# Second attention of a six-layer kernel: four heads at a time in row and column groups of the array, masked by parity, in a written-out loop

## The chip, the cores and the metric

One core of a Trainium2 chip. Times are device microseconds of that core. TensorE (PE) multiplies on a 128 x 128 array and writes PSUM, eight banks of 128 partitions by 2 KB. VectorE (DVE), ScalarE (ACT) and GpSimd (POOL) do the rest; GpSimd works on SBUF alone. SyncE (SP) issues the transfers.

## The reference, cut to what matters

```python
x = x + 0.5 * L0_ffn(layernorm(x))
x = x + L0_attn(layernorm(x))
x = x + 0.5 * L0_ffn(layernorm(x))
x = x + 0.5 * L1_ffn(layernorm(x))
x = x + L1_attn(layernorm(x))        # the second attention
x = x + 0.5 * L1_ffn(layernorm(x))

# L1_attn: B, S, E, H = 4, 256, 512, 32; D = E // H = 16
q, k, v = split(x @ qkv_w + qkv_b)            # each b, s, H, 16
q, k = rope(q), rope(k)
s = einsum('bqhd,bkhd->bhqk', q, k) / 4 + (1 - tril) * -66504
p = softmax(s)
y = einsum('bhqk,bkhd->bqhd', p, v).reshape(b, s, e) @ out_w + out_b
```

x is 4 batches x 256 tokens x 512; all is fp32. The second attention has 4 x 32 = 128 heads of 16 columns.

## The kernel before

The six layers run one after another on x, which stays in SBUF. Each engine has its own instruction list; semaphores order them. Large products run in three fp32r matmuls (`product`, L346: high x high, high x low, low x high) on operands split into a high and a low half; scores, weighted sums and transposes are plain fp32.

The second attention (`b_tensor`, `b_scalar`, `b_vector`, `b_gpsimd`) begins when the feed-forward layer has written all of x. A batch has 256 tokens in two tiles of 128, and 32 heads in four groups of eight (a group is 128 columns of q, k and v). Per batch there are six projections `PROJ` (q, k, v by two token tiles, 12 matmuls each), a bias addition for each (L1564), and for q and k a rotation: cosine on VectorE (L1570), sine on GpSimd (L1675), sum on VectorE (L1578). Per group, `b_tensor_prepare` (L1375) transposes q and k into one bank and VectorE copies them to `qkT` (L1584). ScalarE then makes eight copies of the transposed q, each multiplied by a column of `table` that is one on the 16 partitions of one head and zero elsewhere (`qz`, L1470), and scatters v on the diagonal of a zeroed buffer `vz` (L1481), so that each head's product over all 128 partitions is that head's own.

Head i passes through the engines in steps j: scores(j) (L1396: query tile 0 against 128 keys, tile 1 against 256), minima on VectorE with the causal mask added (L1602, L1605; scores are negated), exponentials with row sums on ScalarE (L1495), the inverse sums a step later (L1612), two products on GpSimd (L1688, L1690), three 128 x 128 transposes three steps later (L1405, into bank PT), a copy to SBUF on VectorE (L1616), and the weighted sum four steps later (L1416, L1418), in which a group's eight heads accumulate into bank OB. A group's result is split by ScalarE (L1502) and VectorE (L1620). TensorE's order within a step is turn(j-3), scores(j), weigh(j-4), then extra work from tables: the next group's transposes, a norm of the next batch, one projection of the next batch at j = 19, 21, ... 29, output products (L1431) at j = 34 to 36. `b_run` runs batches in a loop of the hardware (`Fori`), with 37 steps written out at its start and for the last batch. Banks 0 and 1 take projections and transposed q and k, 2 and 3 scores, 4 the turned probabilities, 5 the weighted sum, 6 and 7 norms and outputs.

In the last batch the weights of the next layer are split as well (L245 on ScalarE, L258 on GpSimd), 11 chunks over 28 steps.

Of the kernel before, what the change touches and what calls it, by code (L numbers as in the profile page):

```python
# [24 lines left out]
P = 128  # L25
# [60 lines left out]
T_FIRST = T_HEAD + HG1  # L86
# [14 lines left out]
def constants():  # L101
# [22 lines left out]
    t[:, T_HEAD:T_HEAD + HG1] = np.arange(P)[:, None] // D1 == np.arange(HG1)[None, :]  # L124
# [4 lines left out]
def program(nc, x_in, w_in, table_in, bias_in, rows_in, out):  # L129
    ctx = ExitStack()  # L130
    with ctx:
# [44 lines left out]
        with ExitStack() as a:  # L176
            qkT = sb(a, "qkT", [P, 2, 2 * SEQ])
# [3 lines left out]
            oT1 = [sb(a, f"oT1_{i}", [P, GR1, SEQ], F32R) for i in (HI, LO)]  # L181
            qkv = sb(a, "qkv", [P, 2, 3 * DIM])
            s1 = sb(a, "s1", [P, 4, 3 * P])
            bqkv = sb(a, "bqkv", [P, 3 * DIM])
# [1077 lines left out]
        b_proj_free = sem("b_proj_free")  # L1262
        b_sin = sem("b_sin")
        b_cos = sem("b_cos")
        b_rope = sem("b_rope")
        b_q = sem("b_q")
        b_v = sem("b_v")
# [6 lines left out]
        b_pt = sem("b_pt")  # L1274
# [3 lines left out]
        b_out = sem("b_out")  # L1278
        b_added = sem("b_added")
        b_zero = sem("b_zero")  # L1280
        LN1 = 32
        TURN_LAG, WEIGH_LAG = 3, 4
        OVER = WEIGH_LAG + 1

        PROJ = [(0, 0), (1, 0), (0, 1), (1, 1), (2, 0), (2, 1)]
        PROJ_AT = {19 + 2 * i: p for i, p in enumerate(PROJ)}
        FILLS1 = GR1 + len(PROJ)


        LN_AT, LAST_LN_AT = {5: 0, 12: 1}, {5: 0, 11: 1, 17: 2, 24: 3}  # L1290
        LAST_SPLIT_AT = {OVER + i * 28 // F1_CHUNKS: i for i in range(F1_CHUNKS)}
        NEXT_AT = 28
        OUTPUTS_AT = {34: [0, 1], 35: [2], 36: [3]}

        def prep_at(j):


            return j // HG1 + 1 if j % HG1 == 0 and j // HG1 % GR1 < GR1 - 1 else None

        def ended_before(j):  # L1300

            i = j - 1 - WEIGH_LAG
            return i // HG1 if i > 0 and i % HG1 == HG1 - 1 else None

        def fill_of(b, what):


            if isinstance(what, int):
                i = what // GR1 * FILLS1 + what % GR1 - 1
            else:  # L1310
                i = GR1 - 1 + FILL_ORDER.index(what)
            n = FILLS1 - 3 + i
            return b * FILLS1 + n, n % 2

        NEXT = "next"
        FILL_ORDER = PROJ[:5] + [NEXT] + PROJ[5:]

        def b_run(eng, step, ahead):

            ahead(-1)  # L1320
            for j in range(OVER):
                step(0, j, True)
            with eng.Fori(0, BATCH - 1) as b:
                for j in range(OVER, HEADS1 + OVER):
                    step(b, j, True)
            for j in range(OVER, HEADS1 + OVER):
                step(BATCH - 1, j, False)

        def there(i, more):

            return 0 <= i and (i < HEADS1 or more)

        def ln_no(b, tt):
            return b * 2 + (LN1 + 2 + tt)


        def b_tensor(pe):
            pe.wait_ge(f_mul, ffn1b.m0)
            st_a1.ready(pe, A1_CHUNKS - 1)
            b_run(pe, lambda b, j, more: b_tensor_step(pe, b, j, more),  # L1340
                  lambda b: b_tensor_ahead(pe, b))

        def b_claim(pe, b, what):
            n, s = fill_of(b, what)
            pe.wait_ge(b_proj_free, n + 1)
            return bank[s]

        def tile_at(j, more):

            return (LN_AT if more else LAST_LN_AT).get(j)  # L1350

        def b_tensor_norm(pe, b, tt):
            pe.wait_ge(b_added, b * 4 + 1)
            ln_turn(pe, ln_no(b, tt), tt % 2, OUTB[tt % 2])

        def b_tensor_project(pe, b, what):
            j, tt = what
            if what == PROJ[0]:
                pe.wait_ge(ln_done, ln_no(b, 1) + 1)
            dst = b_claim(pe, b, what)  # L1360
# [6 lines left out]
        def b_tensor_prepare(pe, b, what):  # L1367
            grp = 0 if what == NEXT else what
            if what == NEXT:
                pe.wait_ge(b_rope, b * 4 + 8)  # L1370
            dst = b_claim(pe, b, what)
            for j in range(2):
                for tt in range(2):
                    c = j * DIM + grp % GR1 * P
                    last = nc.tensor.transpose(dst[:, j * SEQ + tt * P:j * SEQ + (tt + 1) * P],  # L1375
                                               qkv[:, tt, c:c + P], ident)
            last.then_inc(b_proj, 1)

        def b_tensor_ahead(pe, b):
            for what in FILL_ORDER:  # L1380
                if what == NEXT:
                    b_tensor_prepare(pe, b, NEXT)
                else:
                    b_tensor_project(pe, b, what)

        def b_tensor_step(pe, b, j, more):
            def scores(i):
                grp, hh = divmod(i, HG1)
                s = grp % 2
                if hh == 0:  # L1390
                    n = fill_of(b + grp // GR1 - 1, NEXT) if grp % GR1 == 0 else fill_of(b, grp)
                    pe.wait_ge(b_proj_free, n[0] + 3)
                    pe.wait_ge(b_q, b * GR1 + grp + 1)
                pe.wait_ge(b_min, b * HEADS1 + i + 1)
                for qt, n in enumerate((P, 2 * P)):
                    last = nc.tensor.matmul(bank[2 + i % 2][:, qt * P:qt * P + n],  # L1396
                                            qz[:, s, hh, qt * P:(qt + 1) * P],
                                            qkT[:, s, SEQ:SEQ + n], start=True, stop=True)
                last.then_inc(b_scores, 1)

            def turn(i):
                pe.wait_ge(b_norm, b * HEADS1 + i + 1)
                pe.wait_ge(b_pt, b * HEADS1 + i + 1)
                for blk in range(3):
                    last = nc.tensor.transpose(bank[PT][:, blk * P:(blk + 1) * P],  # L1405
                                               s1[:, i % 4, blk * P:(blk + 1) * P], ident)
                last.then_inc(b_turned, 1)

            def weigh(i):
                grp, hh = divmod(i, HG1)  # L1410
                if hh == 0:
                    pe.wait_ge(b_v, b * GR1 + grp + 1)
                    pe.wait_ge(b_o_lo, b * GR1 + grp + 1)
                pe.wait_ge(b_pt, b * HEADS1 + i + 2)

                nc.tensor.matmul(bank[OB][:, 0:SEQ], vz[:, grp % 2, 0, hh, :], pt1[:, i % 2, 0:2 * P],  # L1416
                                 start=hh == 0, stop=False)
# [452 lines left out]
```

## Time and profile before

| | us |
|---|---|
| median of 3 runs | 2020.61 |
| lowest, highest | 2018.2, 2024.47 |
| span of the profiled execution | 2014.8 |
| PE, PEld busy in it | 1872.6, 1655.0 |
| DVE, ACT, POOL busy in it | 1174.6, 1104.2, 881.5 |
| second attention (1575.8 to 1941.3) | 365.5 |

The profile is of one execution; its own time is known as the span from its first to its last instruction, 2014.8, which lies 3.4 us under the lowest run and 5.8 under the median. A matmul record's duration includes the way through the array; how fast matmuls follow each other is read from the chain. An fp32 matmul of scores or weighted sum is two records (256 calls, 512 records).

### The profile page before, as it was taken

What the parts mean: (1) busy time and instruction counts of PE and PEld (TensorE: products, weight loads), DVE (VectorE), ACT (ScalarE), POOL (GpSimd) and SP (SyncE); (2) the same over time, 40 slices, a digit from 0 to 9 for tenths busy, and PEclk for the clock granted to TensorE, in tenths of its full rate; (3) what the DMA queues carried; (4) which work ended last, traced back from release to release, by engine and by line L of the source; (5) the groups of instructions that cost most, each with busy time, mean ns of one, the idle gap of its engine ahead of it and who ended that gap; (6) DMA issues with size and microseconds to landing.
All of it is one profiled execution on the core that took longest, in us unless ns stands there. A gap on an engine that the chain in (4) does not pass through costs nothing.

```text
span 2014.8 us, 35562 instructions
## 1 busy us (share of the span) xinstructions
PE 1872.6 (93%) x11076; PEld 1655.0 (82%) x11076; DVE 1174.6 (58%) x3502; ACT 1104.2 (55%) x3103; POOL 881.5 (44%) x1241
## 2 busy tenths in 40 slices
PE   5979999999999999999999999998988898989888
PEld 4769998988988988988998899997766687878776
DVE  3555565565565466456456556545557675766766
ACT  3336566565566566466656656664325455465744
POOL 5335444444544444444544544542313353545630
PEclk9999999999999999999999999999989999999999
DMA  5200011021011012002002001102111100000101
GB/s 173 68 1 17 17 54 34 7 64 34 1 53 49 1 41 62 1 29 69 6 17 70 17 17 53 33 7 63 37 41 49 42 1 1 0 1 0 38 6 42
DMA packets 35013, 66.12 MB, mean 33 GB/s; under 512 B 3968, under 2 KB 4096, under 8 KB 34816
## 3 DMA queue, kind: packets, MB, share of 16 engines
q1 hardware_dynamic: 34816, 63.74, 10.4%
q8 instruction: 94, 1.54, 0.3%
q14 instruction: 103, 0.84, 0.1%
HBM read 61.62 MB, written 2.10 MB: 32 GB/s over the span
## 4 chain that ended last, share of the span: by engine, by line
PE 76%; DVE 8%; ACT 7%; issue 7%; POOL 2%; DMA 0%; DVEq 0%; ACTq 0%; SPq 0%; POOLq 0%
PE bank L346 56%; PE bank L925 5%; PE bank L912 4%; PE bank L1396 3%; PE bank L927 2%; PE bank L1416 2%; ACT s L1026 2%; PE bank L1405 2%; PE bank L1418 1%; ACT W L245 1%; ACT s L1495 1%; POOL WF L258 1%; DVE h L634 1%; DVE x L1183 1%; PE bank L318 1%
## 5 line engine op out<-in xcount | busy, mean ns | idle before, releaser
L346 PE MATMUL bank<-W,oT 128*128 128x512 f32 x1632 | 434.2, 402 | 0.0
L1224 POOL TENSOR_TENSOR qk<-work,qk 128x512 fp32r<-128x512 f32 (+1 forms) x160 | 189.8, 1186 | 489.7 <-ACT qk L1017 489.7
L346 PEld LDWEIGHTS bank<-W,oT 128*128 128x128 f32 x1632 | 289.4, 190 | 47.5
L1033 ACT COPY pt<-bank 128x384 f32<-128x384 f32 x256 | 121.9, 476 | 342.5 <-PE bank L912 342.0
L1026 ACT ACTIVATE s<-s,neg_max 128x128 f32<-128x128 f32 (+1 forms) x512 | 227.5, 445 | 59.2 <-DVE neg_max L1137 57.7
L1216 POOL TENSOR_TENSOR work<-work,table 128x512 f32<-128x512 f32 (+1 forms) x160 | 160.6, 1004 | 138.4 <-ACT work L1012 138.4
L1495 ACT ACTIVATE s<-s,neg_max 128x128 f32<-128x128 f32 (+1 forms) x256 | 114.3, 447 | 136.8 <-DVE neg_max L1605 136.4
L346 PE MATMUL bank<-W,xnA 128*128 128x320 f32 (+1 forms) x1056 | 186.7, 333 | 1.6 <-DVE qkv L1564 0.8
L1114 DVE TENSOR_TENSOR work<-bank,table 128x512 f32<-128x512 f32 (+1 forms) x160 | 101.9, 637 | 131.7 <-ACT work L1012 131.7
L346 PEld LDWEIGHTS bank<-W,xnA 128*128 128x128 f32 x1056 | 166.4, 188 | 14.2 <-DVE qkv L1564 1.3
L346 PE MATMUL bank<-xnA,W 128*128 128x256 f32 (+1 forms) x1080 | 163.6, 302 | 11.8 <-DVE W L251 6.4
L346 PE MATMUL bank<-qk 128*128 128x256 f32 (+1 forms) x768 | 167.7, 354 | 5.6 <-POOL qk L1224 5.6
L346 PE MATMUL bank<-xnB,W 128*128 128x256 f32 (+1 forms) x1080 | 161.8, 300 | 4.7 <-DVE xnB L331 4.7
L925 PE MATMUL bank<-pt,lvv 128*128 128x256 f32 x512 | 152.8, 379 | 13.1 <-DVE oT L1150 12.4
L1189 DVE COPY lvv<-bank 128x320 f32<-128x320 f32 x128 | 62.9, 492 | 171.8 <-PE bank L346 171.8
L346 PEld LDWEIGHTS bank<-xnA,W 128*128 128x128 f32 x1080 | 143.6, 192 | 21.5 <-DVE W L251 9.5
L1237 POOL TENSOR_TENSOR s<-s,inv_sum 128x256 f32<-128x256 f32 x256 | 156.9, 613 | 0.0
L346 PEld LDWEIGHTS bank<-xnB,W 128*128 128x128 f32 x1080 | 143.1, 191 | 11.5 <-DVE xnB L331 5.6
L912 PE MATMUL bank<-table,s 128*128 128x128 f32 x768 | 126.8, 274 | 9.8 <-issue 8.4
L1017 ACT CAST qk<-work 128x512 fp32r<-128x512 f32 (+1 forms) x160 | 92.4, 578 | 73.3 <-DVE work L1123 72.4
L1235 POOL TENSOR_TENSOR s<-s,inv_sum 128x128 f32<-128x128 f32 x256 | 107.9, 422 | 52.5 <-DVE inv_sum L1145 51.6
L1123 DVE TENSOR_TENSOR work<-work 128x512 f32<-128x512 f32 (+1 forms) x160 | 113.2, 708 | 30.2 <-issue 15.0
(107 smaller groups left out, 3913.3 us busy)
## 6 DMA issues: line engine op xcount, KB each, us to landing
raw<-in_weights SPq DMA_DIRECT2D x215, 256.0 KB, 2.8
x<-in_x SPq DMA_DIRECT2D x8, 256.0 KB, 4.8
out<-x SPq DMA_DIRECT2D x8, 256.0 KB, 2.0
row<-in_bias_rows SPq DMA_DIRECT2D x5, 256.0 KB, 2.7
table<-in_constants SPq DMA_DIRECT2D x1, 960.0 KB, 5.1
bqkv<-in_bias_rows SPq DMA_DIRECT2D x1, 768.0 KB, 4.8
table<-in_constants SPq DMA_DIRECT2D x1, 69.0 KB, 2.4
biases<-in_bias_columns SPq DMA_DIRECT2D x1, 15.0 KB, 2.9
```

Of the source, the lines that this page charges most:

```text
L346: last = nc.tensor.matmul(out_ap, lhs(i), rhs(j), start=start and k == 0, stop=stop and k == 2)
L912: last = nc.tensor.transpose(bank[PT][:, blk * P:(blk + 1) * P], s0[:, s, blk * P:(blk + 1) * P], ident)
L925: nc.tensor.matmul(bank[OB][:, 0:SEQ], lvv[:, 0, col:col + P], pt0[:, k, 0:2 * P], start=True, stop=False)
L1026: last = nc.scalar.activation(s0[:, s, cols], s0[:, s, cols], ACT.Exp, bias=neg_max[:, s, qt:qt + 1], scale=-1.0, accum_out=row_sum[:, s, ...
L1033: nc.scalar.copy(pt0[:, k, :], bank[PT][:, 0:3 * P]).then_inc(a_pt, 1)
L1114: nc.vector.tensor_tensor(work[:, 2 + s, cols], bank[fs][:, cols], table[:, T_COS + cols.start:T_COS + cols.stop], ALU.mult).then_inc(a_pr ...
L1123: nc.vector.tensor_tensor(work[:, 2 + s, cols], work[:, 2 + s, cols], work[:, s, cols], ALU.add).then_inc(a_rope, 1)
L1216: nc.gpsimd.tensor_tensor(work[:, s, cols], work[:, s, cols], table[:, T_SIN + cols.start:T_SIN + cols.stop], ALU.mult).then_inc(a_sin, 1)
L1224: nc.gpsimd.tensor_tensor(lo, work[:, 2 + s, st.columns(what)], hi.bitcast(F32), ALU.subtract).then_inc(a_rope_lo, 1)
L1235: nc.gpsimd.tensor_tensor(s0[:, s, 0:P], s0[:, s, 0:P], inv_sum[:, s, 0:1].to_broadcast([P, P]), ALU.mult)
L1237: nc.gpsimd.tensor_tensor(s0[:, s, P:3 * P], s0[:, s, P:3 * P], inv_sum[:, s, 1:2].to_broadcast([P, 2 * P]), ALU.mult).then_inc(a_norm, 1)
L1495: last = nc.scalar.activation(s1[:, s, cols], s1[:, s, cols], ACT.Exp, bias=neg_max[:, s, qt:qt + 1], scale=-1.0, accum_out=row_sum[:, s, ...
```

## The change

The second attention is written anew, everything else stays. A step is now four heads (a quad, half a group: the even heads of a group or its odd heads); there are 8 quads a batch, 32 in all and two steps to finish, written out for all batches, without `Fori`.

- Scores: q of a group is copied twice instead of eight times, once with the odd and once with the even heads zeroed. Head j of the quad lies on partitions 32j to 32j+31 (its 16 and 16 zeroed ones), and its scores are a matmul over those 32 partitions alone, on row group j, into its own bank j. The four heads' matmuls for query tile 0 come first, then the four for tile 1.
- Weighted sum: v of a head is 32 columns (16 of them zero), on column group j, into partitions 32j to 32j+31 of bank OUT1.
- The zeroed buffer `vz` shrinks from 8 to 2 slots a group and tile, and GpSimd fills it instead of ScalarE. The two products of a head on GpSimd become one of 384 columns, with the inverses written out per block by VectorE, one reciprocal for two heads. Three of four copies of turned probabilities move from VectorE to ScalarE. The addition of the bias row moves from VectorE to GpSimd.
- The turned probabilities have two banks (4, 5). Projections, transposed q and k, norms and output products all go through the one bank FILL (7), in a fixed order: each waits until its predecessor has been copied out.
- The rotation is done in place; q and k of two batches are kept.

```diff
-            qz = sb(a, "qz", [P, 2, HG1, SEQ])
-            vz = sb(a, "vz", [P, 2, 2, HG1, P])
-            pt1 = sb(a, "pt1", [P, 2, 3 * P])
+            qz = sb(a, "qz", [P, 2, 2, SEQ])
+            vz = sb(a, "vz", [P, 2, 2, 2, P])
+            pt1 = sb(a, "pt1", [P, 4, 3 * P])
...
+        SCORE, PTB, OUT1, FILL = (0, 1, 2, 3), (4, 5), 6, 7
+        PROJ_STEP = {1: 0, 2: 1, 3: 2, 4: 3, 7: 4}
+        def middle_use(n):
+            b, s = divmod(n, PER_BATCH)
+            if n >= QUADS:
+                return None
+            if s == 0:
+                return ("proj", b, 5)
+            if s in PROJ_STEP and b + 1 < BATCH:
+                return ("proj", b + 1, PROJ_STEP[s])
+            if s in (5, 6) and b > 0:
+                return ("out", b - 1, s - 5)
+            return None
+        def first_use(n):
...
+            if s == 0:
+                return ("norm", b, 0)
+            if s == 2 and b + 1 == BATCH:
+                return ("norm", b, 2)
+            if s in (1, 3, 5):
+                return ("prep", b, s // 2 + 1)
+            if s == 6 and b + 1 < BATCH:
+                return ("prep", b + 1, 0)
+        def last_use(n):
...
+            if s == 0:
+                return ("norm", b, 1)
+            if s == 2 and b + 1 == BATCH:
+                return ("norm", b, 3)
...
+            def scores():
+                group, odd = divmod(n, 2)
...
+                at_least(pe, b_min, 4 * n)
+                for qt in range(2):
+                    cols = slice(qt * P, qt * P + (qt + 1) * P)
+                    for j in range(4):
+                        last = nc.tensor.matmul(bank[SCORE[j]][:, cols],
+                                                qz[rows(j), group % 2, odd, qt * P:(qt + 1) * P],
+                                                kT[rows(j), group % 2, 0:(qt + 1) * P], start=True, stop=True)
                 last.then_inc(b_scores, 1)
+            def weigh(m):
+                group, odd = divmod(m, 2)
...
+                for s in b_pt:
+                    pe.wait_ge(s, 2 * (m + 1))
+                for tt in range(2):
+                    for j in range(4):
+                        last = nc.tensor.matmul(bank[OUT1][rows(j), tt * P:SEQ],
+                                                vz[:, group % 2, odd, tt, 32 * j:32 * (j + 1)],
+                                                pt1[:, j, tt * 2 * P:(tt + 2) * P],
+                                                start=odd == 0 and tt == 0, stop=odd == 1 and tt == 1)
...
+            if n < QUADS:
+                scores()
+            if n >= 2:
+                weigh(n - 2)
+            b_tensor_fill(pe, first_use(n))
+            if 1 <= n <= QUADS:
+                turn(n - 1, 0)
+                turn(n - 1, 1)
+            b_tensor_fill(pe, middle_use(n))
+            if 1 <= n <= QUADS:
+                turn(n - 1, 2)
+                turn(n - 1, 3)
+            b_tensor_fill(pe, last_use(n))
...
+            if n >= 2 and n % 2:
...
+                act.wait_ge(b_pv, group + 1)
+                nc.scalar.copy(oT1[HI][:, group % ORING, :], bank[OUT1][:, 0:SEQ]).then_inc(b_o_hi, 1)
+            if here:
+                exponentials(0)
+            if first and first[0] == "norm":
+                norm_hi(first)
+            if before:
+                b_pt_copy(act, n - 1, 0)
+            if first and first[0] == "prep":
+                b_scalar_masks(act, *first[1:])
+            if here:
+                exponentials(1)
+            if before:
+                b_pt_copy(act, n - 1, 1)
+            if here:
+                exponentials(2)
+                exponentials(3)
+            if before:
+                b_pt_copy(act, n - 1, 2)
...
```

VectorE's step is minima of heads 0 and 1, the copy of a group's transposed keys, minima of heads 2 and 3, then the low half of a group's result, a norm's low half, the cosine, inverses(0) (heads 0 and 1), the rotation's sum, norm moments, the bias addition or the addition of an output product, norm applications, inverses(1) (heads 2 and 3), the copy of turned head 3 of the quad before. GpSimd's step is products 0 and 1, norm powers, a sine, a group's values, products 2 and 3, a bias row, weight splits.

## Rows read from the trace of the kernel before

**Rows 1.** Windows: start of the second attention, all of it, what follows; us, PE, PEld, DVE, ACT, POOL busy (x), PEclk, DMA.
```profile
...
1575.80:1597.10 21.30, 17.62 (x77) 13.70 (x77) 12.13 (x16) 3.45 (x10) 12.17 (x10) 1.00 0.27 99
1575.80:1941.30 365.50, 325.31 (x1896) 281.67 (x1896) 247.17 (x923) 199.50 (x710) 183.84 (x311) 0.99 0.04 12
1941.30:2014.80 73.50, 61.99 (x262) 47.95 (x262) 50.63 (x84) 32.63 (x53) 3.70 (x4) 0.97 0.09 33
...
```

**Rows 2.** Waits in 1575.8 to 1941.3: engine line <- releaser: total, times, longest.
```profile
...
POOL s L1688 <- DVE inv_sum L1612: 162.9, 102, 8.9
ACT s L1495 <- DVE neg_max L1605: 136.4, 115, 4.6
...
DVE s L1602 <- PE bank L1396: 26.0, 62, 2.8
...
```

**Rows 3.** The chain, four stretches of the stage: start us, us, what.
```profile
...
1692.29 2.72 issue
...
1703.08 0.45 PE bank L1375 x4
...
1713.37 0.33 PE bank L1405 x3
1713.70 0.66 PE bank L1396 x4
1714.36 0.43 PE bank L1416 x2
1714.79 0.22 PE bank L1418 x2
...
1726.20 2.77 PE bank L346 x12
...
```

**Rows 4.** Groups by shape in 1575.8 to 1941.3: count | busy us, mean ns | idle before.
```profile
...
L1690 POOL TENSOR_TENSOR s<-s,inv_sum 128x256 f32<-128x256 f32 x128 | 84.1, 657 | 0.0
...
L346 PE MATMUL bank<-W,xnA 128*128 128x512 f32 x288 | 71.2, 398 | 1.1 <-DVE qkv L1564 0.8 <-DVEq L1533 0.3
...
L1396 PEld LDWEIGHTS bank<-qkT,qz 128*128 128x128 f32 x512 | 68.6, 195 | 9.9 <-issue 7.8 <-DVE qkv L1564 1.9 <-DVE neg_max L1605 0.2
...
L1470 ACT ACTIVATE qz<-qkT,table 128x256 f32<-128x256 f32 x128 | 60.2, 496 | 24.4 <-DVE qkT L1584 24.4
...
L1688 POOL TENSOR_TENSOR s<-s,inv_sum 128x128 f32<-128x128 f32 x128 | 53.3, 417 | 163.1 <-DVE inv_sum L1612 162.9
...
L1396 PE MATMUL bank<-qkT,qz 128*128 128x128 f32 x256 | 50.7, 280 | 8.4 <-ACT qz L1470 6.7 <-DVE qkv L1564 1.5 <-issue 0.2
...
L258 POOL TENSOR_TENSOR W<-raw,W 128x512 fp32r<-128x512 f32 x11 | 14.0, 1272 | 5.8 <-ACT W L245 5.8
...
L245 ACT CAST W<-raw 128x512 fp32r<-128x512 f32 x11 | 6.7, 606 | 0.0
...
```

**Rows 5.** Timeline of one head's minima and exponentials: start us, us, engine.
```profile
...
1705.32 0.28 DVE L1602 CUSTOM_DVE_ANT_0 s<-bank,table 128x128 f32<-128x128 f32 x1
...
1705.87 0.16 DVE L1612 RECIPROCAL inv_sum<-row_sum 128x2 f32<-128x2 f32 x1
...
1705.99 0.40 ACT L1495 ACTIVATE s<-s,neg_max 128x128 f32<-128x128 f32 x1 [0.43 <-DVE neg_max L1605]
...
1706.88 0.49 ACT L1470 ACTIVATE qz<-qkT,table 128x256 f32<-128x256 f32 x1
...
```

**Rows 6.** The page, part 5: the same copy of turned probabilities in the first attention.
```profile
...
L1033 ACT COPY pt<-bank 128x384 f32<-128x384 f32 x256 | 121.9, 476 | 342.5 <-PE bank L912 342.0
...
```

**Rows 7.** Windows of TensorE alone, 1673 to 1682, 1930 to 1932: us, PE busy (x), PEclk.
```profile
...
1673.60:1675.70 2.10, 0.00 (x0) 1.00 0.00 0
1676.50:1679.90 3.40, 3.40 (x15) 0.50 0.00 0
1680.00:1682.00 2.00, 2.00 (x14) 1.00 0.04 12
1930.00:1932.00 2.00, 0.58 (x5) 1.00 0.01 4
...
```

More of the change, by code:

```diff
@@ L85 @@
 T_HEAD = T_MH + 2
[L86 removed]
+T_FIRST = T_HEAD + 2
 T_M0 = T_FIRST
@@ L1315, in program @@
[L1315 to L1331, printed above, removed]
@@ L1337, in b_tensor, with proj_bank, prep_bank @@
+        def proj_bank(b, i):
+            return bank[(0, 1, 2, 3, 0)[i]] if b == 0 and i < 5 else bank[FILL]
+        def prep_bank(b, g):
+            return bank[1] if b == 0 and g == 0 else bank[FILL]
         def b_tensor(pe):
@@ L1339, in b_tensor, with b_tensor_project @@
             st_a1.ready(pe, A1_CHUNKS - 1)
[L1340 to L1360, printed above, removed]
+            for i in range(5):
+                if i == 4:
+                    pe.wait_ge(b_biased, 1)
+                b_tensor_project(pe, 0, i)
+            pe.wait_ge(b_biased, 2)
+            b_tensor_prepare(pe, 0, 0)
+            for n in range(STEPS1):
+                b_tensor_step(pe, n)
+            fill_released(pe, ("out", BATCH - 1, 0))
+            b_tensor_out(pe, BATCH - 1, 0, bank[FILL])
+            b_tensor_out(pe, BATCH - 1, 1, bank[SCORE[0]])
+        def b_tensor_project(pe, b, i):
+            j, tt = PROJ[i]
+            pe.wait_ge(ln_done, LN1 + 2 * b + tt + 1)
+            dst = proj_bank(b, i)
             for c in range(KC):
@@ L1490, in b_scalar_step, with b_scalar_masks @@
[L1490 to L1493 removed]
+            b_scalar_masks(act, 0, 0)
+            for n in range(STEPS1):
+                b_scalar_step(act, n)
+        def b_scalar_masks(act, b, g):
+            group = GR1 * b + g
+            act.wait_ge(b_k, group + 1)
+            for odd in range(2):
+                last = nc.scalar.activation(qz[:, group % 2, odd, :], prep_bank(b, g)[:, 0:SEQ], ACT.Copy,
+                                            scale=table[:, T_HEAD + odd:T_HEAD + odd + 1])
+            last.then_inc(b_q, 1)
@@ L1519, in b_scalar_step, with norm_hi @@
-            if more and 0 <= j - NEXT_AT - 1 < 3:
-                i = j - NEXT_AT - 1
-                b_scalar_queries(act, b, NEXT, range(3 * i, min(3 * i + 3, HG1)))
-            if more and j == NEXT_AT + 3:
-                b_scalar_values(act, b, NEXT)
+            def norm_hi(use):
+                kind, b, i = use
+                ln_hi_part(act, norm_no(b, i), FILL, xn_tile(i))
+            first, last = first_use(n), last_use(n)
+            here, before = n < QUADS, 1 <= n <= QUADS
@@ new lines, in b_vector_step @@
+            first, middle, last = first_use(n), middle_use(n), last_use(n)
+            roped = middle_use(n - 1) if n else None
+            roped = roped if roped and roped[0] == "proj" and roped[2] < 4 else None
+            here, before = n < QUADS, 1 <= n <= QUADS
+            if here:
+                minima(0)
+                minima(1)
+            if first and first[0] == "prep":
+                b_vector_keys(dve, *first[1:])
+            if here:
+                minima(2)
+                minima(3)
@@ new lines, in b_vector_step @@
+            if here:
+                inverses(0)
+            if roped:
+                b_vector_turned(dve, *roped[1:])
+            if norms_after(n):
+                b_vector_moments(dve, *norms_after(n))
+            if middle and middle[0] == "proj":
+                b_vector_biased(dve, *middle[1:])
+            if middle and middle[0] == "out":
+                b_vector_added(dve, *middle[1:], bank[FILL])
+            if norms_after(n):
+                b_vector_apply(dve, *norms_after(n))
@@ L1658, in b_gpsimd @@
+            if here:
+                inverses(1)
+            if before:
+                b_pt_copy(dve, n - 1, 3)
+            if last:
+                norm_lo(last)
         def b_gpsimd(pool):
```

528 lines of the change are left out of this document (252 added, 276 removed).

## The prediction

> **What bounds the stage now.** The diff touches only the second attention, so I first cut it out with the view by windows. It runs from 1575.8 to 1941.3, 365.5 us of the span of 2014.8; the 73.5 us behind it and the 1575.8 ahead of it keep their code [rows 1]. In it TensorE is busy 325.3 us, VectorE 247.2, ScalarE 199.5, GpSimd 183.8, at a granted clock of 0.99. Next the waits: GpSimd waits 162.9 us for the inverses, ScalarE 136.4 for the minima, VectorE 26.0 for the scores [rows 2]. All three wait for what comes from TensorE. The chain shows why: a head costs TensorE 0.33 us (three transposes), 0.66 (two score matmuls), 0.43 and 0.22 (weighted sum), 1.64 in all, one head right behind the other [rows 3]. 128 heads are 210 us; 24 projections and 8 output products (12 matmuls each [rows 4], 2.76 us [rows 3]) are 88; transposes of queries, keys and norms some 12. That is 310 of the 365.5. The other 55 are the start (21.3 [rows 1], of which 16.6 projections), waits at the change of a group, and loop ends, one of which stands in the chain as 2.72 us of "issue" [rows 3].
>
> **What TensorE gains.** Four heads now share the array: eight score matmuls on row groups 32j, eight weighted-sum matmuls on column groups 32j. The count does not fall: per head still two of each. What falls is time only if neighbours in different groups run at once. No matmul on a part of the array is in this trace, so I bound it.
> - No overlap: scores 4 x 0.66 = 2.6 us for four heads, weighted sum the same, as now.
> - Full overlap: 0.66 each, the time of one.
> - Between: the profile shows two matmul records for each fp32 matmul written (512 weight records for 256 calls [rows 4], and as many matmuls), so each group gets two in a row. If TensorE takes them strictly in order, the second record of group j holds up group j+1 until the first has streamed: only this second and the next group's first overlap. Four groups then take 5 beats instead of 8: 5/8 x 2.6 = 1.6 us.
>
> I take 1.6 for each, as it needs no reordering and is near the middle. The Trainium skill (TensorE: Matmul & The Clock Gate, Part 3) says that matmuls start and end in program order and that four row tiles of one matmul each gave 3.07x; by that figure scores and sum would take some 0.85 each. It gives no such figure for fp32 in two records; no row here shows either.
>
> Three times a step the array changes its division. A 128-column record lasts 0.28 us [rows 4] where the transposes follow each other at 0.11 [rows 3], so emptying the array may cost 0.17, 0.5 a step; nothing is the other bound. I take 0.5, since the trace has no reason why it should be free. The Trainium skill (TensorEngine Tiling (Array Packing), Tiling Modes) says that a change of mode drains TensorE, which speaks against this change. With the drain the sum below stands as it is; without one it would be some 12 us lower (25 steps by 0.5).
>
> TensorE's work for a quad is then 1.77 + 1.77 + 12 transposes 1.32 + 0.17 = 5.0 us (6.6 before).
>
> **What the other engines need.** ScalarE: exponentials of one head take 0.89 (start to start [rows 5]), so 3.6 for four; three of four copies of the turned probabilities move to it, 3 x 0.48 [rows 6]; together 5.0. The eight masked query copies of a group (0.49 each [rows 4]) become two; the copies of the values go to GpSimd. VectorE: minima 0.55 a head [rows 5], 2.2, one copy 0.55, two inverses 0.3, and the rotation. GpSimd: 128 and 256 columns take 0.42 and 0.66 [rows 4], by that slope 384 in one take 0.9; 3.6 a step, plus sines (1.9 a projection), value copies, row additions: up to 7.7 in the fullest step, 5.5 on average. Its products are wanted only a step later, so it stays hidden under 7 us and more. If its cover goes (steps of 6), the fullest cost 1.7 more. What is queued behind the new waits: on TensorE, the projection's wait for FILL holds the transposes of heads 2 and 3 and the next scores, for which VectorE waits; on ScalarE, the wait for the weighted sum holds the exponentials.
>
> **The steps.** 32 steps of four heads. Let 0 be the start of the weighted sum of two steps ago; minima start about there too. The critical order is: probabilities of head 0 copied out by ScalarE behind exponentials 0, then exponentials 1, copy, exponentials 2 and 3; then inverses and the last copy on VectorE (0.7), which releases the next weighted sum and stands ahead of the next minima.
> - Empty even step: exponentials 0 end 1.55; turned at 1.77 + 0.33 + 0.27 = 2.4; copy 2.85, exponentials 3.75, copy 4.2, two more 6.0, plus 0.7: 6.7 us. Odd: ScalarE has the group's result (0.35) ahead of exponentials 0 and waits there for the weighted sum (1.95): 7.55.
> - With a projection or output product and nothing else TensorE sets it: 5.0 + 2.8 = 7.9.
> - With the next group's queries as well (three or four steps in eight): they go into the one bank FILL, and the projection waits until ScalarE has written both masked copies. In an odd step: exponentials 0 end 3.25, copy 3.7, masks 4.6; TensorE has nothing from 2.9 to 4.65; projection 7.4, transposes 8.1, scores 9.9. Even: 9.5. Without a projection 8.45 and 8.05.
> - Step 0 of a batch: transposed norm, its two copies, projection, its bias addition (6.9 to 7.55), second norm, all through FILL: 9.9. Step 7: both norms' moments and applications stand ahead of VectorE's second inverses, and their power behind GpSimd's products: 9.2.
>
> A middle batch: 9.9 + 9.9 + 7.9 + 9.9 + 7.9 + 9.9 + 9.5 + 9.2 = 74.2. The first has no output products and no sums in its first two steps: 68.7. The last has few projections, but two more norms and the 11 weight splits, now in seven steps (1.0 us of ScalarE and 2.0 of GpSimd in each, by 0.61 and 1.27 [rows 4], behind their work of the step; SP's loads wait for them as before, and no other transfer moves): 70. Start: the first scores wait for four biased and rotated projections (4 x 2.8, a sine of 1.9, rotation, transposes, masks): 18 instead of 21.3. End: two steps without scores, two output products (5.5), addition: 14. Sum 18 + 68.7 + 148.4 + 70 + 14 = 319 us against 365.5: 46 less. Writing the loop out removes its ends, which is in these numbers. The profiled span of 2014.8 lies 5.8 under the median of the runs, 2020.6; that rest stays. Forecast 2020.6 - 46 = 1974.
>
> **Rivals.**
> - *Full overlap.* In some 25 steps that TensorE sets, 2 x 0.95 goes, in 7 others 0.9, at the end 1.9: 56 us more, 1918. For it: moving columns are the whole cost of a matmul here. Against: two records a group in order. With steps of 6 to 8 us TensorE is under half busy in some, so part may come back as clock. The Trainium skill (TensorEngine Tiling (Array Packing), Overview) states up to 4x for a small dimension of 32 or less, which speaks for this one.
> - *No overlap, the change does not do what it says.* Scores and sum cost 2.6 each: 2.0 more in the 25 steps, 1.2 in the others, 59 more: 378, slower by 12, 2033. It ends on the other side: TensorE's work is then that of today, and FILL's waits are added to it. It decides once scores and sum cost over 2.4 each. For it: fp32 comes in several passes, whose weights may not be loadable beside a running group (weight records of 0.19 us [rows 4] for matmuls of 0.11 apart).
> - *The clock.* After 2.1 us without a matmul the granted clock was 0.50 for 3.4 us, 1.2 in place of 2.4 GHz [rows 7]; a head then took about 3.3 us instead of 1.64. The new steps have gaps of 1 to 1.7 us in FILL's waits and 1 to 2 in empty steps. Ten falls at 2 us: +20, 1994; in every step +60, which would eat the gain. Against: after two microseconds with 0.58 us of matmuls in them it stayed at 1.00 [rows 7]. The twelve emptiest steps are the risk.
> - *VectorE, not TensorE, is late* (sequence of inverses and copies, wait for FILL longer than seen): 0.5 us a step, +16, 1990. The Trainium skill (TensorEngine Tiling (Array Packing), Performance Considerations) expects this: after tiling, the copies out of PSUM may set the pace. In the empty steps above they do.
>
> **How the numbers follow.** Pairwise overlap as summed: 0.45 (its own range 1950 to 2000). Full or nearly full: 0.25 (1895 to 1950). No overlap: 0.15 (2015 to 2050). Clock or late VectorE on top: 0.15 (1985 to 2015). A measurement of this kernel tells about 0.3%, 6 us. Faster: 0.45 + 0.25 + 0.13 = 0.83; slower 0.13, same 0.04. The range reaches from the full overlap into no overlap: 1900 to 2030 leaves out the ends of both, under 2 in 10.
>
> **What would show it.** In the new profile: the stage under 325 us; the eight score records of 128 columns over 0.55 us (0.86 without overlap, 0.22 with all of it), those of 256 over twice that; TensorE idle before projections in steps with queries, released by ScalarE's masks; ScalarE's idle before exponentials falling from 137 us to under 60; no row of loop ends. Wrong it would be if the records of neighbouring groups stand one behind the other, if the clock in the stage falls under 0.95, or if GpSimd's products release TensorE's transposes in most steps.

## The result and the profile after

The changed kernel takes 1936.4 us (median of four runs, 1935.3 to 1938.3) against 2020.1 for the kernel before on the same chip (2018.2 to 2024.5): ratio 0.960, 95% interval 0.958 to 0.962. The profiled execution has a span of 1934.2 us and a time of 1936.0. The forecast was 1974 with a range of 1900 to 2030; faster was right, the gain is 84 us where 46 were forecast. One run of the kernel before (5135.0 us) and one of values_first (2246.1) stand far above all others and are left out of every ratio and of the median of values_first.

First the stage by windows in the changed kernel (its first 20 us, all of it, what follows; columns as in [rows 1]):

```profile
...
1578.70:1599.00 20.30, 14.84 (x65) 11.78 (x63) 12.48 (x20) 0.94 (x3) 8.79 (x10) 0.89 0.30 104
...
1578.70:1862.50 283.80, 229.56 (x1897) 168.15 (x1895) 176.79 (x756) 183.13 (x678) 169.29 (x223) 0.90 0.05 15
1862.50:1934.20 71.70, 60.55 (x262) 46.81 (x262) 50.55 (x84) 32.63 (x53) 3.71 (x4) 1.00 0.09 34
...
```

283.8 us instead of 365.5: the stage has 81.7 of the 84. TensorE is busy 229.6 us where it was 325.3, with 1897 matmul records in place of 1896. Its granted clock fell from 0.99 to 0.90; with 0.5 as the lower of the two levels that is 0.1 / 0.5 = 0.2 of the stage, some 57 us at 1.2 GHz.

The groups by shape in the stage show what the records of the new form and the moved work cost:

```profile
...
L1440 PE MATMUL bank<-kT,qz 32*128 32x256 f32 x256 | 21.4, 406 | 0.0
L1440 PE MATMUL bank<-kT,qz 32*128 32x128 f32 x256 | 17.0, 337 | 1.5 <-ACT qz L1495 1.5
...
L1454 PE MATMUL bank<-pt,vz 128*32 128x128 f32 x256 | 15.4, 309 | 0.0
...
L1749 POOL TENSOR_TENSOR s<-s,b_inv_sum 128x384 f32<-128x384 f32 x128 | 107.4, 860 | 83.4 <-DVE b_inv_sum L1662 83.0
...
L1760 POOL COPY vz<-v 128x128 f32<-128x128 f32 x32 | 8.6, 299 | 0.0
...
L1502 ACT COPY pt<-bank 128x384 f32<-128x384 f32 x96 | 45.1, 469 | 17.3 <-PE bank L1465 17.2
...
```

256 score records with a mean of 337 ns, and yet only 17.0 us of busy time: 256 x 0.337 would be 86. One record takes no less time than before (280 ns in [rows 4]); several of them run at the same moment. In the step whose scores start at 1640.72 four score records are under way at 1640.76 and eight at 1640.96, by windows of 1 ns.

The timeline of TensorE alone in one step of the second batch (start, length, engine and line, count of records):

```profile
...
1687.91 0.82 PE L1465 MATMUL bank<-table,s 128*128 128x128 f32 x6
1688.65 0.94 PE L1440 MATMUL bank<-kT,qz 32*128 32x128 f32 x16
1689.52 0.86 PE L1454 MATMUL bank<-pt,vz 128*32 128x256 f32 x16
1690.31 0.66 PE L1399 MATMUL bank<-table,qkB 128*128 128x128 f32 x4
1690.80 0.82 PE L1465 MATMUL bank<-table,s 128*128 128x128 f32 x6
1692.86 3.02 PE L350 MATMUL bank<-W,xnA 128*128 128x512 f32 x12 [1.24 <-ACT qz L1495]
...
```

Start to start, the scores of four heads take 0.87 us and the weighted sum 0.79; before, that was 4 x 0.66 and 4 x 0.65 [rows 3]. The last row is the wait that the forecast described: the queries go through FILL, and the projection stands 1.24 us behind ScalarE's masked copies.

Waits in the stage (in total, times, longest):

```profile
...
POOL s L1749 <- DVE b_inv_sum L1662: 83.0, 43, 4.4
...
ACT s L1509 <- DVE b_neg_max L1654: 27.2, 17, 2.6
...
PE bank L350 <- ACT qz L1495: 13.6, 11, 1.4
PE bank L1454 <- DVE pt L1502: 13.3, 14, 2.1
...
DVE s L1651 <- PE bank L1440: 8.9, 19, 0.9
...
```

ScalarE waited 136.4 us for minima and now waits 27.2, VectorE waited 26.0 for scores and now 8.9 [rows 2]. Instead TensorE waits: for the masks, and for the turned probabilities. The chain through a step without a projection (step 5 of the first batch, its steps counted from 0) shows who sets the pace there:

```profile
...
1641.90 0.89 PE bank L1454 x16
1642.82 0.38 ACT oT L1523
1643.19 0.88 ACT s L1509 x4
1644.07 0.36 ACT pt L1502
1644.43 0.74 ACT qz L1495 x2
1645.18 0.86 ACT s L1509 x4
1646.04 0.37 ACT pt L1502
1646.41 1.77 ACT s L1509 x8
1648.32 0.52 DVE pt L1502
...
1648.97 1.45 PE bank L1454 x16
...
```

Of 7.07 us between two of TensorE's rows, 5.4 are ScalarE's: the copy of a group's result, exponentials, copies of turned probabilities and masked queries, one behind the other. 0.5 are VectorE's last copy. TensorE is no longer the bound in such a step. In the step ahead of it, which has a projection and no queries, TensorE waits only 0.24 us: the two engines are nearly even there.

### The profile page after: what moved, and what is told of

It is laid out like the page before. It is cut to its first block, busy times and chain, and to the rows that moved or that the text cites. A ratio compares the mean times of both kernels' runs of the same rounds, so it can differ in the third digit from the quotient of the medians.

```text
span 1934.2 us, 34615 instructions
## 1 busy us (share of the span) xinstructions
PE 1773.3 (92%) x11076; PEld 1539.3 (80%) x11076; DVE 1106.9 (57%) x3334; ACT 1088.1 (56%) x3071; POOL 899.9 (47%) x1153
## 4 chain that ended last, share of the span: by engine, by line
PE 71%; ACT 9%; DVE 8%; issue 6%; POOL 3%; DMA 1%; DVEq 0%; ACTq 0%; SPq 0%; POOLq 0%
PE bank L350 56%; PE bank L929 5%; PE bank L916 4%; PE bank L931 2%; ACT s L1509 2%; ACT s L1030 2%; PE bank L1454 1%; ACT W L249 1%; PE bank L322 1%; PE bank L1465 1%; DVE x L1187 1%; POOL WF L262 1%; POOL rstd L315 1%; DVE work L649 1%; DVE h L638 1%
## 5 line engine op out<-in xcount | busy, mean ns | idle before, releaser
L1030 ACT ACTIVATE s<-s,neg_max 128x128 f32<-128x128 f32 (+1 forms) x512 | 227.7, 446 | 51.0 <-DVE neg_max L1141 50.2
L1220 POOL TENSOR_TENSOR work<-work,table 128x512 f32<-128x512 f32 (+1 forms) x160 | 191.9, 1200 | 134.3 <-ACT work L1016 134.3
L350 PE MATMUL bank<-W,xnA 128*128 128x320 f32 (+1 forms) x1056 | 190.9, 338 | 11.9 <-ACT qz L1495 7.7
L350 PEld LDWEIGHTS bank<-xnB,W 128*128 128x128 f32 x1080 | 143.2, 191 | 11.4 <-DVE xnB L335 5.6
L1749 POOL TENSOR_TENSOR s<-s,b_inv_sum 128x384 f32<-128x384 f32 x128 | 107.4, 860 | 83.4 <-DVE b_inv_sum L1662 83.0
```

Of the source, the lines that this page charges most:

```text
L350: last = nc.tensor.matmul(out_ap, lhs(i), rhs(j), start=start and k == 0, stop=stop and k == 2)
L1030: last = nc.scalar.activation(s0[:, s, cols], s0[:, s, cols], ACT.Exp, bias=neg_max[:, s, qt:qt + 1], scale=-1.0, accum_out=row_sum[:, s, ...
L1220: nc.gpsimd.tensor_tensor(work[:, s, cols], work[:, s, cols], table[:, T_SIN + cols.start:T_SIN + cols.stop], ALU.mult).then_inc(a_sin, 1)
L1749: nc.gpsimd.tensor_tensor(blocks, blocks, b_inv_sum[:, at, 1:4].unsqueeze(2).to_broadcast([P, 3, P]), ALU.mult).then_inc(b_norm, 1)
```

## The experiments

All runs, each against the kernel before on its own chip (there 2018.5 to 2022.8 us); the stage is that of the profiled execution, from its first projection to the first matmul behind it.

| kernel | median us | ratio to before, 95% interval | stage us | clock in stage |
|---|---|---|---|---|
| before | 2020.1 | 1 | 365.5 | 0.99 |
| changed | 1936.4 | 0.960 (0.958 to 0.962) | 283.9 | 0.90 |
| full_both | 2027.2 | 1.004 (1.001 to 1.006) | 374.7 | 0.97 |
| full_scores | 1975.9 | 0.978 (0.973 to 0.982) | 323.4 | 0.94 |
| full_sums | 1995.4 | 0.987 (0.982 to 0.992) | 346.2 | 0.94 |
| by_head | 1939.7 | 0.960 (0.956 to 0.964) | 286.5 | 0.89 |
| written_out | 2010.7 | 0.995 (0.992 to 0.997) | 359.2 | 1.00 |
| warm | 1930.4 | 0.956 (0.952 to 0.960) | 277.3 | 0.98 |
| early | 1927.7 | 0.954 (0.950 to 0.958) | 272.5 | 0.92 |
| early_warm | 1921.1 | 0.950 (0.945 to 0.954) | 267.6 | 0.99 |
| after_again | 1934.9 | 0.959 (0.957 to 0.961) | 283.9 | 0.90 |
| early_again | 1924.3 | 0.955 (0.952 to 0.957) | 270.0 | 0.94 |
| early_warm_start | 1922.2 | 0.952 (0.950 to 0.954) | 272.6 | 0.92 |
| values_first | 1917.0 | 0.949 (0.946 to 0.953) | 266.2 | 0.98 |

### Does the gain come from groups that run at once?

The first theory is that nearly all of the gain is that matmuls in different groups of the array run together; the rival, that the order of the steps and the loop written out bring it. Three kernels put the scores, the weighted sum or both back on the whole array, with the same number of matmuls and moving columns; the operands are then four times as high or wide, and a quad's eight sums accumulate in one place, with `start` at the first and `stop` at the last:

```
-  qz[rows(j), group % 2, odd, qt * P:(qt + 1) * P], kT[rows(j), group % 2, 0:(qt + 1) * P]
+  qz[:, group % 2, odd, qt * P:(qt + 1) * P], kT[:, group % 2, 0:(qt + 1) * P]      # full_scores
-  bank[OUT1][rows(j), tt * P:SEQ], vz[:, group % 2, odd, tt, 32 * j:32 * (j + 1)]
+  bank[OUT1][:, tt * P:SEQ], vz[:, group % 2, odd, tt, :]                           # full_sums
```

**full_both**

> Scores and weighted sums are issued on the whole array again (128 partitions, 128 columns), as many matmuls as in the changed kernel and in the same order; scores become sums over the heads of a quad and the weighted sum lands on all partitions, so the values differ. Theory A, the gain comes from groups of the array running at once: the eight matmuls of the scores take 2.6 us again instead of 0.77, those of the sums 2.6 instead of 0.7; TensorE needs 9.3 us in a step with a projection; the stage takes 350 to 370 us and the program 2000 to 2020. Theory B, the gain comes from the rest (loop written out, copies and products moved, no group changes): the stage stays under 310 us, the program under 1960.

**full_scores**

> Only the scores are on the whole array again (values differ as they then sum over the quad's heads). Theory A: 1.9 us more in each of some 22 steps in which TensorE has a projection or an output product, nearly nothing in the others, since the scores are issued ahead: 1936 + 40 = 1976 us. Theory B: within 10 us of 1936.

**full_sums**

> Only the weighted sums are on the whole array again (each head's sum lands on all partitions, so values differ). Theory A: the sum stands in the chain of every step (copies, sum, transposes, copies), so 1.9 us more in nearly all 32: 1936 + 50 to 60 = 1990 us, more than for the scores. Theory B: within 10 us of 1936.

With both on the whole array the kernel takes 2027.2 us, 0.4% more than before, and its stage 374.7, both somewhat over what was expected of the groups' theory. Put back alone, the scores give 1975.9 (40 more than the changed kernel) and the weighted sum 1995.4 (59 more). TensorE's timeline of full_both in a step without a projection:

```profile
...
1649.17 0.38 PE L1466 MATMUL bank<-table,s 128*128 128x128 f32 x2
1649.39 2.79 PE L1440 MATMUL bank<-kT,qz 128*128 128x128 f32 x16
1652.02 2.78 PE L1454 MATMUL bank<-pt,vz 128*128 128x256 f32 x16
1654.63 0.60 PE L1399 MATMUL bank<-table,qkB 128*128 128x128 f32 x4
...
```

Start to start 2.63 and 2.61 us for what takes 0.87 and 0.79 in groups: 1.76 and 1.82 less a step. At most three of these score records are under way at once, looked at every 0.08 us. In the stage, scores in groups are worth 374.7 - 346.2 = 28.5 us as long as the sum is on the whole array, the sum 374.7 - 323.4 = 51.3, and both together 90.8, or 2.84 for each of 32 steps. That is more than their sum. Most of the excess stands in the step at the start of a batch: step 0 of the second batch takes 12.3 us in full_both and still 12.3 in full_sums, 10.3 in full_scores and 9.0 in the changed kernel. Why it does was not tried. The order of the steps without the groups brings nothing; the rival of the experiment falls.

### Does the order in which the matmuls are issued matter?

The forecast took 1.6 us for four heads because each group has two records in a row, and a strict order would let only neighbours overlap. by_head makes the runs longer: the loops over heads and query tiles change places, so that each group has four records in a row.

```
-                for qt in range(2):
-                    for j in range(4):
+                for j in range(4):
+                    for qt in range(2):
```

> The scores are issued head by head (tile 0 then tile 1 of a head, then the next head), so that each row group gets four records in a row instead of two. If TensorE took matmuls strictly in order, only the last record of a head could overlap the first of the next: 4 x 0.64 - 3 x 0.11 = 2.2 us for the scores of a quad instead of 0.77, and the program about 30 us longer, 1966. If each group takes its own matmuls as it becomes free, the scores still take 0.8 us and the program 1936, within 6.

The kernel takes 1939.7 us, the same ratio as the changed kernel, and the scores as long:

```profile
...
1640.49 0.38 PE L1465 MATMUL bank<-table,s 128*128 128x128 f32 x2
1640.80 0.96 PE L1440 MATMUL bank<-kT,qz 32*128 32x128 f32 x16
...
```

0.96 us against 0.94. If a group's later records held up the next group, this order would cost clearly more than the other. The strict order in groups falls: in this kernel, how many records of one group stand in a row (two or four) makes no difference that shows.

### What is the loop, written out, worth?

written_out is the kernel before with its loop over the batches unrolled and nothing else changed.

```
-            with eng.Fori(0, BATCH - 1) as b:
+            for b in range(BATCH - 1):
```

> This is the kernel before with its loop over the batches written out and nothing else changed. The theory that writing the loop out is a small part of the gain: the chain of waits of the kernel before shows a loop end as 2.72 us of issue; two or three of them go, so 5 to 8 us less, about 2013 to 2015. The rival, from the run with whole-array scores and sums (2027.2 against 2020.1, that is all of the gain lies in the groups running together): the loop ends lie under work of other engines or TensorE's queue runs ahead over them, so within 0.3% of 2020.

The ratio is 0.995 (0.992 to 0.997), some 11 us, and the stage is 359.2 us instead of 365.5, so 6.3 less in the stage; the rest lies ahead of it or is spread of the runs, and its cause stays open. The theory holds in size, and the forecast read its row rightly: the kernel before has two such loop ends (2.72 and 2.76 us in the chain), in which VectorE stands for 2.3 us with nothing named that it waits for, and written_out has neither:

```profile
...
1784.36 0.56 DVE L1616 COPY pt<-bank 128x384 f32<-128x384 f32 x1 [2.33 <-issue]
...
```

Behind them the kernel before ran at half clock for some 3 us each (0.51 in 1697.4 to 1700.4); written_out has no such stretch there. Another wait stays in both kernels, once a batch, where the first scores of a new batch are due. In the profile of the kernel before TensorE waits 2.23 us for ScalarE's masked queries; in that of written_out the wait has no name, but TensorE starts 0.1 us behind the last of the same copies:

```profile
...
1675.75 0.99 PE L1396 MATMUL bank<-qkT,qz 128*128 128x128 f32 x4 [2.23 <-ACT qz L1470]
...
1765.67 0.89 ACT L1470 ACTIVATE qz<-qkT,table 128x256 f32<-128x256 f32 x2
...
1766.67 0.89 PE L1396 MATMUL bank<-qkT,qz 128*128 128x128 f32 x4 [2.20 <-issue]
...
```

The first row is of the kernel before, the others are of written_out. Against this kernel, full_both costs 374.7 - 359.2 = 15.5 us in the stage. So the edit is two things: groups, worth 91 us, and a new order of work with masks and FILL, which costs 15 and gets 6 back from the loop.

### What does the lower clock cost?

TensorE ran at 1.2 GHz for some 57 us of the changed kernel's stage. The longest stretch is at the start, where TensorE waits for the first rotated queries. The window on it, and the rows of TensorE's timeline there:

```profile
...
1594.50:1608.00 13.50, 7.31 (x32) 5.20 (x33) 8.07 (x30) 6.22 (x20) 3.27 (x5) 0.50 0.00 0
...
```

```profile
...
1596.40 1.09 PE L1399 MATMUL bank<-table,qkB 128*128 128x128 f32 x4 [3.96 <-DVE qkB L1606]
1599.03 1.67 PE L1440 MATMUL bank<-kT,qz 32*128 32x128 f32 x16 [1.54 <-ACT qz L1495]
1600.77 1.09 PE L322 MATMUL bank<-table,work 128*128 128x128 f32 x4
1604.53 4.68 PE L350 MATMUL bank<-W,xnA 128*128 128x512 f32 x12 [2.67 <-DVE xnA L335]
...
```

warm adds 42 matmuls (84 records) that nobody reads into TensorE's waits, so that the clock stays up:

```
+        def b_tensor_warm(pe, count, to=OUT1):
+            for _ in range(count):
+                nc.tensor.matmul(bank[to][:, SEQ:SEQ + 256], ident, table[:, T_M1:T_M1 + 256],
+                                 start=True, stop=True)
...
+            b_tensor_warm(pe, 8)      # ahead of the first turned queries
...
+            if n < 2:
+                b_tensor_warm(pe, 6 if n == 0 else 2)
```

> The kernel after, with some 70 matmuls of 256 columns that nobody reads, put into TensorE's waits of the emptiest steps and of steps 0 and 1. In the kernel after TensorE's granted clock is 0.90 in the stage, some 57 us of it at half. The theory that the half clock costs time: the granted clock in the stage rises to 0.97 or more and the stage (283.8 us) gets 8 to 15 us shorter, 1922 to 1928 in all. The rival that it lies in waits and costs nothing: the clock rises and the time stays within 6 us of 1936, or gets longer by what the added matmuls hold up (up to 10 us).

The clock in the stage rises to 0.98, the stage is 277.3 us, 6.6 less (8 to 15 were expected), and the kernel takes 1930.4. The interval of its ratio overlaps that of the changed kernel, so the whole time alone does not decide; the steps do. In the same place, in warm:

```profile
...
1600.19 0.94 PE L1451 MATMUL bank<-kT,qz 32*128 32x128 f32 x16 [0.24 <-ACT qz L1523]
...
1605.70 3.02 PE L350 MATMUL bank<-W,xnA 128*128 128x512 f32 x12 [0.54 <-DVE xnA L335]
...
```

The projection takes 3.02 us instead of 4.68, and step 0, from one start of scores to the next, 9.9 instead of 11.6, step 1 7.7 instead of 9.3. In the second batch nearly nothing changes (7.8, 7.2, 7.8, 5.9 against 7.8, 7.1, 7.8, 5.9), and in the last the added matmuls make two steps longer (by 1.3 and 1.7 us) and three shorter (by 0.4 to 1.4). So the half clock costs where a projection is on the path, and hardly anything in steps that ScalarE sets. The third batch fits this: its step 0, which holds a projection, takes 10.3 us in warm, and 11.2 in the changed kernel, where the clock fell in it.

### What does the wait for the masks cost?

early sends the turned queries and keys of groups 2 and 3 and of the next batch's group 0 as the last use of FILL in an even step, behind its projection instead of ahead of the next one, and puts their copies first in the next step of VectorE and ScalarE.

```
-            if s in (1, 3, 5):
-                return ("prep", b, s // 2 + 1)
...
+            if s == 2:
+                return ("prep", b, 2)
+            if s == 4:
+                return ("prep", b, 3)
...
+            earlier = last_use(n - 1) if n else None
+            if earlier and earlier[0] == "prep":
+                b_scalar_masks(act, *earlier[1:])
```

> The kernel after, with the transposed queries and keys of groups 2 and 3 and of the next batch's group 0 sent as the last use of FILL in the step before, and the masked copies first in ScalarE's next step. TensorE's wait for ScalarE's masked copies ahead of a projection (up to 1.4 to 1.6 us, 11 of them) goes. The theory that this wait lies on the path: 10 to 15 us less, 1921 to 1926. The rival that ScalarE and VectorE set these steps and TensorE only waits elsewhere: within 6 us of 1936; ScalarE's exponentials then start 1 us later in the steps with masks.

> Both edits of the two runs before in one kernel. If both costs lie on the path and do not overlap, the gains add: 18 to 30 us less than the kernel after, 1906 to 1918. If the early queries leave longer empty waits and the clock falls there, the added matmuls are worth more here than alone; if neither lies on the path, 1930 to 1946.

early takes 1927.7 us, and the stage 272.5, 11.4 less. TensorE's waits for the masked copies ahead of projections are 3 with 3.8 us in all, where they were 11 with 13.6, and the projection follows the transposes at once:

```profile
...
1683.90 0.86 PE L1462 MATMUL bank<-pt,vz 128*32 128x256 f32 x16
1684.68 0.87 PE L1473 MATMUL bank<-table,s 128*128 128x128 f32 x6
1685.32 3.01 PE L350 MATMUL bank<-W,xnA 128*128 128x512 f32 x12
1688.16 0.82 PE L1473 MATMUL bank<-table,s 128*128 128x128 f32 x6
...
```

early_warm, with both edits, takes 1921.1 and its stage 267.6: 16.3 less than the changed kernel, where the edits alone give 6.6 and 11.4. They nearly add (18.0), but the kernel takes 3 us more than the upper end of what was expected for it (1906 to 1918).

To compare on one chip, three kernels ran together: the changed one, early, and early with added matmuls only ahead of and in steps 0 and 1.

> The changed kernel itself once more, so that the three kernels of this call can be compared on one chip: 1936 us within 0.3%.

> The kernel with the queries and keys sent a step early, beside the changed kernel on the same chip. If the waits for the masked copies lie on the path: 8 to 12 us under the changed kernel. If the difference of the first look came from the chip: the same time.

> Queries and keys a step early, and added matmuls only ahead of and in steps 0 and 1 of the first batch. In the kernel with all the added matmuls the steps of the second and third batch were as long as in the one with none (10.3, 7.8, 7.9, 5.9 in both), and those of the last were longer. The theory that of all the half clock only that at the stage's start costs time: about 1919, 5 to 8 us under the kernel with early queries alone. The rival that the later half clock costs too: about 1925, 4 us over the kernel with all of them (1921).

The changed kernel gives 1934.9 and early 1924.3, 10.6 less, and their intervals lie apart. That the wait for the masks lies on the path is shown. early_warm_start gives 1922.2 (0.950 to 0.954), which cannot be told from early; of the two theories on the later half clock neither is settled by the times. Its profile speaks for the second: the clock fell again behind the start of the second and third batch, and step 0 there took 11.2 and 11.4 us, against 10.3 and 10.3 in early_warm; both are steps with a projection behind a wait. Which step is hit differs between executions of nearly the same code.

### Is GpSimd hidden?

The forecast had GpSimd under cover. Three times in the stage the weighted sum of a group waits 1.20 us for it. All engines in the changed kernel:

```profile
...
1681.74 1.40 POOL L1734 TENSOR_TENSOR work<-qkB,table 128x256 f32<-128x256 f32 x2 [1.08 <-DVE qkB L1594]
...
1683.09 0.52 POOL L1760 COPY vz<-v 128x128 f32<-128x128 f32 x2
...
1683.66 0.42 PE L1454 MATMUL bank<-pt,vz 128*32 128x256 f32 x4 [1.20 <-POOL vz L1760]
...
```

The values were there at 1673.07, when VectorE had added their bias; their copy stands in GpSimd's queue behind two products, whose inverses come at 1679, and behind a sine that waits for a projection. values_first is early_warm with this copy first in the step:

```
+            if n < QUADS and s in VALUES_AT:
+                values(VALUES_AT[s])
             if n < QUADS:
                 normalise(0)
...
-            if n < QUADS and s in VALUES_AT:
-                values(VALUES_AT[s])
```

> The kernel with early queries and all the added matmuls, and besides GpSimd copies a group's values first in its step instead of behind two products and the sine. In the changed kernel and in that with early queries the weighted sum of each batch's group 0 starts 1.20 us late, released by this copy (three times). The theory that this copy is late by its place in GpSimd's queue, contrary to the forecast, which had GpSimd hidden: the wait goes, three or four times 1.2, so 3.6 to 4.8 us less than with both edits, about 1917, and the stage under 265 (267.6). The rival that VectorE or ScalarE is right behind it in that step: the wait changes its releaser and the stage stays at 267.

The steps in question take 6.6 and 6.7 us instead of 7.9 each, as expected, and TensorE no longer waits for that copy. The stage is 266.2 and not under 265: in this execution step 0 of the second and of the last batch, at the lower clock, took 0.9 and 1.1 us longer than in early_warm. 1917.0 us is the lowest median of all kernels, but its difference to early_warm (4.2) is less than the intervals can tell. Against the changed kernel the ratio is 0.949 / 0.960 = 0.989.

## Why the prediction was too high

- **What bounds the stage.** Right. With the groups taken away and all else kept, the stage is 374.7 us; the forecast for "no overlap" was 378. That it is off by only 3 us is in part luck: the two middle batches took 85.4 each where the forecast's steps, with its 2.0 more in each, give 90.2; the start (20.3 for 18) and the first and last batch, longer than forecast, make up for it.
- **Scores and weighted sum of four heads, 1.6 us each.** This is the step that failed. "Pairwise overlap" was argued from the two records of each matmul and a strict order; measured are 0.87 and 0.79 start to start, with the emptying of the array in both. The array comes near the bound "full overlap" (0.66): without the emptying, priced below, it is 2.63 / (0.87 - 0.09) = 3.4 times as fast. The forecast's 0.45 for pairwise and 0.25 for full overlap were the wrong way round. The sign it named was poorly set: 128-column score records are busy 17.0 us / 32 steps = 0.53, just under the 0.55 named and far from the 0.22 of full overlap, because a record lasts longer than its columns stream (0.28 at a spacing of 0.11 [rows 3, 4]), which that figure left out; the distance from start to start shows it. By full overlap the sum of the forecast was 56 less, a stage of 263 and 1918 us in all: 1936 lies between the two, nearer to that one. That it lies in the range is owed to the range's width and not to the sum.
- **A change of the array's division, 0.17 each.** It was mis-sized. Behind the last transpose of a step the scores start 0.20 us later (1640.52 to 1640.72); in full_both, without a change of division, 0.11 (1649.28 to 1649.39, the second of the x2 in its first row). Nearly all steps of both kernels show these two distances. 0.09 for this change; if the two others of a step cost the same, which no row shows by itself, that is 0.28 instead of 0.5. The Trainium skill (TensorEngine Tiling (Array Packing), Tiling Modes) says that a change of mode drains TensorE; the trace agrees that there is a cost, and it is small beside the 3.6 us that the groups give.
- **Steps.** Taking 1.9 off each forecast step of a middle batch, as that rival does, gives 74.2 - 15.2 = 59.0 (its eight steps as listed add up to 74.1); the second batch took 59.5 and the third 61.6. Single steps differ: 7.1 where 6.0 was due, with the 1.20 for the values, and 5.9 where 7.3 was due at the batch's end.
- **The clock.** The rival was real but not alone: 0.90 in the stage, under the 0.95 that the forecast named as a sign of being wrong. It was priced at 20 us for ten falls at 2 us each. Keeping it up gave 6.6 us net of what the added matmuls cost, half of it in the first two steps. The first batch took 65.7 us where the same subtraction gives some 55 (its first two steps have no weighted sum); these 10 are about half of the 21 us between 263 and 284. In warm it took 60.9, with 3.3 of the 4.8 less in steps 0 and 1. Its last step took 9.5 us in the changed kernel, 8.6 in warm and 6.5 in early: in the changed kernel the clock was at half for most of it, and its projection took 4.36 us instead of 3.0; in early the clock stayed up there.
- **FILL's waits.** Right in place, and in size nearly: 11 waits, up to 1.4 us where 1.75 was forecast. Removing all but three gave 10.6 us.
- **GpSimd.** Products 0.86 us where 0.9 was estimated, but not hidden everywhere: the order in its queue cost 1.2 three times.
- **Loop ends.** The row was read rightly. The forecast gave them no number; writing out the loop gave 6.3 us in the stage.
- **Start and end.** 20.3 us for 18 and 13.6 for 14. On the chain of the start stands the load of the biases: VectorE waits 5.26 us for it, until 1584.9.
- **VectorE late.** It is part of the path in empty steps, as the forecast said, but most of what lies there is ScalarE's.

## What to carry to other kernels

When matmuls have a small dimension of 32, put four of them into separate row or column groups and count on nearly the time of one, fp32 with its two records included (0.87 and 0.79 us here for what took 2.6, one alone 0.66); then work out who is next, because a step that TensorE no longer sets is set by the exponentials and copies. Spend the array's free time on the order around it: a shared bank that a slow copy has to leave, or a ready copy behind a late one in an engine's queue, matters once TensorE is fast: the early queries, the clock kept up and the early values together gave one per cent. To price such an edit, run it once with the groups widened to the whole array, since this splits the gain of the array from the cost of the new order.

## What the runs showed that was not expected

- Records of all four groups overlap although each is longer than before (337 ns against 280), and two or four records of one group in a row make no difference (0.94 and 0.96 us for sixteen).
- The gains of scores and sum in groups are 28.5 and 51.3 us alone but 90.8 together.
- The granted clock was at half for some 57 of 284 us, and keeping it up (0.98) gave only 6.6.
- A wait can lose its name from one profile to the next: the 2.2 us at each change of batch is put down to ScalarE's masked queries in the kernel before and stands as "issue" in written_out, though it ends behind the same copies.
